# Running the last mixture-of-experts layer of three images inside the next image's attention, and mixing narrow key tiles among full ones

## What is computed

```python
def _L3_attn_ref(x, W1, b1, w2, b2):              # x = layernorm(t)
    f = jnp.einsum('bih,ha->bia', x, W1[:h])      # a: 16
    g = jnp.einsum('bjh,ha->bja', x, W1[h:])
    tt = jnp.tanh(f[:, :, None, :] + g[:, None, :, :] + b1)
    scores = jnp.einsum('bija,a->bij', tt, w2[:, 0]) + b2[0]
    e = jnp.exp(scores) * strictly_lower_triangle
    w = e / (jnp.sum(e, axis=-1, keepdims=True) + 1e-10)
    return jnp.einsum('bij,bjh->bih', w, x)

def _L3_ffn_ref(x, router_w, router_b, expert_w, expert_b):   # x = layernorm(t)
    p = softmax(x @ router_w + router_b)          # 8 experts, the best 2 kept
    top_p, top_i = jax.lax.top_k(p, 2); top_p = top_p / top_p.sum(-1)
    out = jnp.einsum('bnd,edc->bnec', x, expert_w) + expert_b
    return the top_p-weighted sum of the two chosen experts

t = t + _L3_attn_ref(_ln_t(t), ...)
t = t + _L3_ffn_ref(_ln_t(t), ...)
x = t.transpose(0, 2, 1).reshape(4, 128, 64, 64)
```

## Time and profile before

| | us |
|---|---|
| median of three runs | 8764.21 (8760.24 to 8766.25) |
| the profiled execution, its own time | 8764.93 |
| its span, first to last instruction | 8763.1 |
| layers 0 to 2, in the span | 0 to about 4298 |
| attention of layer 3 | 4299.6 to 8378 |
| experts of layer 3 | 8379 to about 8707 |
| way out | about 8709 to 8763 |
| busy share of the span | PE 78%, DVE 73%, ACT 64%, POOL 33% |

### The profile page before, as it was taken

The page is one execution under the profiler, slowest core; times in us unless marked ns, Lnnn a source line. Parts: engine busy times, 40 slices in busy tenths (PEclk is TensorE's granted clock), DMA queues, the critical chain, the costliest instruction groups (busy, mean ns, idle before and its releaser), DMA issues. The chain is left out here.

```text
span 8763.1 us, 103094 instructions
## 1 busy us (share of the span) xinstructions
PE 6793.0 (78%) x37512; PEld 2460.3 (28%) x37512; DVE 6439.3 (73%) x10840; ACT 5612.2 (64%) x4625; POOL 2881.3 (33%) x2218
## 2 busy tenths in 40 slices
PE   8999999987886169948876767777777767767688
PEld 3333333323443123314321213221222212212144
DVE  6777777776754643357888888888888888888766
ACT  3222222214554342234699999999999999999954
POOL 5655566630000300005431223231322223213255
PEclk9999999987887579978989999999999999999998
DMA  1000000001010000000000000000000000000000
GB/s 47 1 1 1 1 1 1 1 4 27 23 26 4 7 0 0 0 0 3 3 1 1 1 1 1 1 1 1 1 1 1 1 1 1 1 1 1 1 3 39
DMA packets 23728, 45.12 MB, mean 5 GB/s; under 512 B 10219, under 2 KB 13421, under 8 KB 22127
## 3 DMA queue, kind: packets, MB, share of 16 engines
q1 hardware_dynamic: 23278, 39.11, 1.5%
HBM read 13.92 MB, written 8.39 MB: 3 GB/s over the span
## 5 line engine op out<-in xcount | busy, mean ns | idle before, releaser
L2350 ACT ACTIVATE aa_tanh<-aa_tanh 128x4096 f32<-128x4096 f32 (+8 forms) x1280 | 3699.3, 2977 | 133.5 <-DVE aa_tanh L2479 133.3
L2479 DVE TENSOR_SCALAR aa_tanh<-aa_f_times,aa_g_bias 128x1024 f32<-128x1024 f32 (+19 forms) x5120 | 3307.6, 718 | 634.2 <-PE aa_scores L2389 633.2
L2389 PE MATMUL aa_scores<-aa_tanh,aa_w_spread 128*32 128x512 f32 (+8 forms) x18432 | 2204.7, 596 | 997.3 <-ACT aa_tanh L2350 996.4
L2318 POOL TENSOR_TENSOR aa_denominators<-aa_denominators,aa_weights 128x1024 f32<-128x1024 f32 (+7 forms) x304 | 771.1, 2536 | 2132.5 <-ACT aa_weights L2341 2122.8
L2389 PEld LDWEIGHTS aa_scores<-aa_tanh,aa_w_spread 128*32 128x32 f32 x18432 | 598.0, 113 | 2454.0 <-ACT aa_tanh L2350 1533.3
L278 POOL TENSOR_TENSOR near_tap_weights<-near_hat_y_mask,near_hat_x 128x1024 f32<-128x1024 f32 x400 | 937.6, 2367 | 473.8 <-PE near_weights_spread L570 465.2
L584 PE MATMUL near_out_sum<-near_weighted,near_w_out 128*128 128x512 f32 x1984 | 997.9, 626 | 24.4 <-DVE near_weighted L357 13.9
L570 PE MATMUL near_weights_spread<-near_tap_weights,near_spread_consts 36*64 36x512 f32 x6272 | 799.3, 609 | 19.3 <-DVE near_weighted L357 12.9
L2403 PE MATMUL aa_out_sum<-aa_weights,aa_normed 128*128 128x512 f32 (+3 forms) x1152 | 598.7, 641 | 148.7 <-POOL aa_weights L2313 148.7
L346 DVE TENSOR_TENSOR near_weighted<-near_weights_spread,near_values 128x1024 f32<-128x1024 f32 x496 | 589.5, 1220 | 147.4 <-PE near_weights_spread L570 147.4
L346 DVE TENSOR_TENSOR near_weights_spread<-near_weights_spread,near_values 128x1024 f32<-128x1024 f32 x288 | 354.0, 1229 | 336.9 <-PE near_weights_spread L570 336.9
(11 more groups left out here) (332 smaller groups left out, 7239.2 us busy)
## 6 DMA issues: line engine op xcount, KB each, us to landing
l_taps<-l_scan_in_out SPq DMA_DIRECT2D x256, 64.0 KB, 2.0
x_rows<-in_x SPq DMA_DIRECT2D x4, 2048.0 KB, 14.3
out_x<-x_rows SPq DMA_DIRECT2D x4, 2048.0 KB, 6.3
qa_x<-in_L_attn_w SPq DMA_DIRECT2D x1, 1024.0 KB, 5.7
L_ffn_expert_w<-in_L_ffn_expert_w SPq DMA_DIRECT2D x2, 512.0 KB
near_spread_consts<-in_deform_consts SPq DMA_DIRECT2D x1, 805.5 KB, 8.2
aa_weights_in<-in_attention SPq DMA_DIRECT2D x1, 577.5 KB
l_weights<-in_mamba SPq DMA_DIRECT2D x1, 557.0 KB
```

The costliest lines, as they stand in the source:

```text
L2318: pool.tensor_tensor(DEN[:, lo:CHUNK], DEN[:, lo:CHUNK], ET[:, n % 2, 0:w], ALU.add).then_inc(den_added, 1)
L2350: a.activation(TH[:, tt, 0:length], TH[:, tt, 0:length], ACT.Tanh).then_inc(th_ready, 1)
L2389: last = t.matmul(sp_[32 * q:32 * q + 32, n % 2, s:e], W2S[:, tt, :], TH[:, tt, o + s:o + e], start=tt == 0, stop=tt == 3, tile_position=( ...
L2479: last = v.tensor_scalar(TH[:, tt, at[q]:at[q] + w - s], FR[:, m % 2, lo + s:CHUNK], GB[:, key:key + 1], None, ALU.add)
```

## The change

The attention stage becomes `attention_and_experts`. It does four things.

1. **The experts of images 0 to 2 run inside the attention of images 1 to 3.** The tables `behind`, `choose` and `raise_gates` give places (n, tt) to new jobs. A *group* is 4 token tiles, eight to an image. Per group: `mt` (4 transposes of the normalised tokens, from GpSimd's `normalize_group`), `ml` (router logits), 8 times `e` (one matmul for 4 experts of one token tile) and `x` (4 transposes back to channels by rows, which replaces the way out). A new group starts every 11 steps (`PERIOD`), so groups overlap and each step of the stretch has one job. They share the two spare banks, in the same rotation, with the own jobs. VectorE does its part four steps of the order later: after `e` it adds all four experts itself (`add_experts`, four chained `scalar_tensor_tensor`), so that it does the work of ScalarE and GpSimd in `moe_layer` too. The gating has the same 18 steps, on 32 columns rather than 128, once per group. Jobs stand only at full key tiles, from the fifth key tile of chunks c = 1 to 3 on: 106 steps of an image, 16 in c = 1, 40 in c = 2, 50 in c = 3.
2. **Diagonal key tiles are spread** (`key_order`): c = 0 takes D0, D7, D1, D6, D2, D5, D3, D4; c = 3 takes 0, D0, 1, 2, 3, D1, 4, 5, 6, D2 and so on; c = 1 and c = 2 likewise. `exponents` comes after step 3 where the tile is narrower than 512.
3. **The norm before the experts is done per image**, with one square root for each, at the start of chunk c = 1 of the next image.
4. `moe_layer` and `to_channels` are left with image 3 alone (32 token tiles, 4 turns of the loop). The outputs of images 0 to 2 are stored by SyncE during the attention, and the expert weights are loaded at its start (three more DMAs, waited for by VectorE before its first instruction on them).

```diff
@@ moe_layer
-        NCK, NGRP = TT // CK, TT // 4
+        NTL = TT - first
+        NCK = NTL // CK
...
+GE = 4 * EX
+STEPS, PERIOD = 18, 11
+NGI = NT // 4
...
-        tiles = [(m, j) for m in range(NM) for j in range((m % NCH + 1) * CT_)]
...
+        def key_order(c):
+
+            if c == 0:
+                return [0, 7, 1, 6, 2, 5, 3, 4]
+            order = list(range(c * CT_))
+            for k in range(CT_ - 1, -1, -1):
+                order.insert(min(c * k + 1, 7 * c), c * CT_ + k)
+            return order
+
+        tiles = [(m, j) for m in range(NM) for j in key_order(m % NCH)]
...
+        behind, choose, raise_gates = {}, {}, {}
+        for b in range(NB - 1):
+            at = [(n, tt) for n, (m, j) in enumerate(tiles) for tt in range(4)
+                  if m // NCH == b + 1 and j < m % NCH * CT_ and 4 <= n - first_of[m] < (m % NCH + 1) * CT_ - 5]
+            for g in range(NGI):
+                G, p = b * NGI + g, PERIOD * g
+                behind[at[p]], behind[at[p + 3]] = ("mt", G), ("ml", G)
+                for k, o in enumerate((1, 2, 4, 5, 7, 8, 9, 10)):
+                    behind[at[p + PERIOD + o]] = ("e", 8 * G + k)
+                behind[at[p + 2 * PERIOD + 6]] = ("x", G)
+                for o, steps in ((4, range(0, 4)), (5, range(4, 8)), (6, range(8, 12)), (9, range(12, 15)), (10, range(15, STEPS))):
+                    choose[at[p + o]] = (G, steps)
+                raise_gates[at[p + 8]] = G
...
@@ gpsimd
+            def normalize_group(G):
+
+                if G % NGI == 0:
+                    pool.wait_ge(sh_ready, 1 + G // NGI + 1)
+                if G:
+                    pool.wait_ge(*full("mt", G - 1))
+                for k in range(4):
+                    t = 4 * G + k
+                    last = pool.tensor_scalar(MU[:, k * P:(k + 1) * P], T[:, t * P:(t + 1) * P], N.scale[:, t:t + 1], SH1[:, t % NT:t % NT + 1], ALU.mult, ALU.add)
+                last.then_inc(mu_ready, 1)
...
@@ scalar
-                    if n and tt == 2:
+                    if n and tt == (2 if w >= BANK else 3):
                         exponents(n - 1)
+                    if (n, tt) in raise_gates:
+                        a.wait_ge(diff_ready, 1 + raise_gates[n, tt] + 1)
+                        a.activation(M1[:, :], M2[:, :], ACT.Exp).then_inc(raised, 1)
+                    if m > NCH and m % NCH == 1 and j == 0 and tt == 1:
+                        N.scalar(a, vv, ss, m // NCH, (m // NCH - 1) * NT, m // NCH * NT)
...
@@ tensor
+            def experts(E):
+
+                G, k, h = E // 8, E % 8 // 2, E % 2
+                t.wait_ge(*bank_before("e", E))
+                t.matmul(bank("e", E), MT[:, G % 2, k * P:(k + 1) * P], EWC[:, 4 * h:4 * h + 4, :].rearrange("p e c -> p (e c)"), start=True, stop=True).then_inc(full("e", E)[0], 1)
...
@@ vector
+            def add_experts(E):
+
+                G, k, h = E // 8, E % 8 // 2, E % 2
+                x = T[:, (4 * G + k) * P:(4 * G + k + 1) * P]
+                v.wait_ge(*full("e", E))
+                if h:
+                    v.wait_ge(*free("e", E - 1))
+                for e in range(4):
+                    c = k * EX + 4 * h + e
+                    ins = v.scalar_tensor_tensor(x, bank("e", E)[:, e * P:(e + 1) * P], GT_[:, G % 2, c:c + 1], x, ALU.mult, ALU.add)
+                    if e < 3:
+                        sum_ch(ins)
+                    else:
+                        ins.then_inc(free("e", E)[0], 1)
...
@@ build
-        additive_attention_layer(nc, d, X, C, N)
-        moe_layer(nc, d, X, C, N, "L3_ffn_", False)
-        to_channels(nc, X, C, out)
+        attention_and_experts(nc, d, X, C, N, out)
+        moe_layer(nc, d, X, C, N, "L3_ffn_", False, TT - NT)
+        to_channels(nc, X, C, out, NB - 1)
```

More of the change, by code:

```diff
@@ new lines, in _ @@
+                    name, at = behind.get((n - 1, tt), (None, 0))
+                    if name == "mt":
+                        keep_group(at)
+                    elif name == "ml":
+                        keep_logits(at)
+                    elif name == "e":
+                        add_experts(at)
+                    elif name == "x":
+                        keep_back(at)
+                    G, steps = choose.get((n - 1, tt), (0, ()))
+                    for step in steps:
+                        gating(G, step)
```

301 lines of the change are left out of this document (229 added, 72 removed).

## The result

The changed kernel takes **8803.55 us** (median of 5 runs, 8798.84 to 8810.66), and the kernel before, on the same chip, 8764.21 (8760.24 to 8768.56). The ratio is **1.0045 [1.0032, 1.0058]**: it is slower by 39 us. The forecast was 8616, faster by 148, with a range to 8735. The time lies outside it, and its sign is the wrong one.

The account below looks back on a forecast made before the run. ScalarE was taken to bound the attention, VectorE having 160 us free per image. 8764.9 - 264.2 (removed work) + 144 (landed jobs) - 40 (spreading) + 8.7 + 3 (small additions) gave 8616 us after a 0.7 median correction; range 8495 to 8735.

Parts of the forecast that it names:

- jobs landed, tables, start: Attention: +144 for experts' jobs landing in three images, +8.7 for square roots with table changes, +3 for the start.
- diagonals spread: Attention, four images: spreading narrow tiles recovers 10 us of ScalarE's loss per image (bounds 0 and 31), -40 in all.
- What goes: Experts stage loses 228.6 us, way out 34.6, norm at the join about 1: together -264.2.
- The slack of the diagonal tiles: Attention: VectorE has 0.85 us free at each diagonal tile, so 12 between the jobs' tiles absorb 10 per image.
- Jobs landed: Images 1 to 3: of VectorE's 151 us added per image, 48 land on the path (bounds 25 and 80), +144.
- The stall of the normalising: Attention: VectorE's fills stand still during GpSimd's `normalize_group`, taken as 1.5 us per group of four token tiles.
- `raise_gates`: Attention: ScalarE waits for VectorE to be two steps further, but is faster there and makes it up; no cost.
- Small additions: Attention: +8.7 for three square roots, +3 for a later start; gates' exps, stores and TensorE's extra work cost nothing.
- All hidden: Rival, attention: VectorE is ahead enough, ScalarE stays the bound and no jobs land; 8477 us, chance 0.15.
- GpSimd's stalls shrink: Rival, attention: GpSimd adds starting while VectorE reads a bank stall nothing; 8576 us, chance 0.15.
- Bank rotation: Rival, attention: TensorE waits for spare banks with scores queued behind, so all 151 us land per image; 8925 us, chance 0.12.
- TensorE's clock: Rival, attention: TensorE's granted clock falls to 0.6 and its work exceeds ScalarE's pace; 8994 us, chance 0.03.

Follow-up runs that it names:

- e1: Kernel before with only its diagonal key tiles spread, no experts' jobs, exps after step 2: 8893.02 us, ratio 1.0149.
- e5: Changed kernel with the exps back after step 2 for narrow tiles too: 8786.90 us, ratio 1.0018.
- e3: Changed kernel with TensorE's `add_tile` issued two steps later, behind the next tile's step 1: 8724.53 us, ratio 0.9951.
- e4: Changed kernel with key tiles in sequence and a new group every 15 steps instead of 11: 8655.85 us, ratio 0.9874.
- e12: e4 with half of VectorE's expert adds left out for images 0 to 2 and the gates' exp three steps later: 8522.31 us, ratio 0.9722.
- e2: Changed kernel with its key tiles in their old sequence, all else as changed: 8718.16 us, ratio 0.9948.
- e6: e4 with the exp of the gates three steps later and the gating's last pieces with it: 8640.85 us, ratio 0.9859.
- e9: e4 with two instead of four of VectorE's adds per expert matmul for images 0 to 2: 8582.39 us, ratio 0.9787.

## Why the prediction was wrong, point by point

With e1 the 34.2 us between the two profiled spans can be split by the prediction's own sum. The end part is measured at 8666.7 and 8367.8; up to there e1 takes 123.9 more than before; the rest of the 298.9 stands with the jobs. That rest has the later exps in it, since e1 has its exps after step 2.

| term | predicted | measured |
|---|---|---|
| experts stage, way out, norm | -264.2 | -264.7 |
| jobs landed, tables, start | +155.7 | +175.0 |
| diagonals spread | -40 | +123.9 |
| sum | -148.5 | +34.2 |

By the medians the parts are 126.6 (e1), 20.7 for the later exps (e5), 156.7 for the jobs (e5 against e1, and 264.7 that go) and -264.7, together 39.3.

**What goes: right.** The pace of 38.10 per set and of 2.88 per turn carried over; 97 and 24 were forecast for what is left, and 98.0 and 22.3 are its windows.

**Diagonals spread: the failed step.** It had 0 to 31 us gained per image, and no loss among its bounds. It counted the fill (2.7) and the narrow tile's cover (under 2), and left out what stands between them. Three things do: the last full step's scores on TensorE (1.92), `add_tile` queued behind them (1.98), and the stall behind GpSimd's add that the late fill then meets (4.91 for four fills of 2.7). The stall was in the same prediction, for full tiles, but not carried to this place. The ordering of TensorE's queue was, for the jobs, but not for `add_tile`. e3 shows the mechanism, since moving these matmuls alone gives back 81, some 55 more than in an order without spreading, and takes the cost in image 0 from 29 to 7. There is one thing more behind it: VectorE's lead of four *steps* was read as a lead of time. Four full steps are 15 us, four steps of D6 about 4. Spread tiles cut the lead each time they come, the narrow tail of the kernel before once per chunk.

**The slack of the diagonal tiles** (0.85 each, from a difference of busy times) was correct as a mean and had no meaning at a place. A mean of free time does not say that a transfer of work between neighbours fits.

**Jobs landed: right in mechanism, near in size.** 48 were foretold to land per image besides 2.9 for the tables. The 175 are 58 for each with the later exps, and 52 without them (156.7); between image 1 and image 0 of the same kernel the chunks c = 1 to 3 grow by 4.5, 24.7 and 20.4, together 49.6. It was a matter of VectorE's free time at the full tiles, as reckoned: e4 shows it by thinning the jobs out and e12 by halving their adds. VectorE's busy time rose by 133.3 us per image and not by 151. Part of that is only how it is counted: one add takes 0.349, but they start 0.38 apart, and the busy time leaves out the gaps between small instructions, by the trace some 12 us in image 1. The 0.366 was about right. The stall of the normalising (1.5 for each of 24 groups, 36) was wrong: the 48 full fills that lie inside an instruction of `normalize_group`, with no add near, took 0.744 each. So a little less work came, and a little more of it landed. The size holds for this order alone: in sequence, e2, the same jobs land 70.

**`raise_gates`: dismissed wrongly.** "ScalarE is the faster one there and makes it up" is true while VectorE is the bound: e6 got 17 of 112 us (three images of 37.2) back. Where it is not, e12 against e9, the same edit is worth 59. In the kernel as changed it was covered, so that this costs the forecast little.

**The exps after step 3** were given no price. They cost 21.

**Small additions.** ScalarE's busy time in image 1 rose by 6.6 (982.4 to 988.9), where the forecast had 2.9 for the tables and eight exps of 0.2. The start was right: from the first DMA of the stage (4294.73 after, 4299.55 before) to ScalarE's first `tanh` (4315.59 and 4316.65) it takes 20.9 us instead of 17.1, 3.8 more where 3 were taken. VectorE now waits for the last of the new loads:

```profile
4301.31 0.68 DVE L2745 TENSOR_SCALAR aa_w_spread<-consts_sb,aa_weights_in 128x32 f32<-128x32 f32 x4 [6.31 <-DMA aa_router_in<-in_experts]
```

**The rivals.** *All hidden* is out: `tanh` waits 92.6 us in the period of one image. *GpSimd's stalls shrink* is out in its size: the fills' busy time over the span rose by 12.7 where it should have fallen. Stalls do fall elsewhere, on small instructions of the gating. VectorE and GpSimd of the kernel after in c = 3 of image 1:

```profile
6107.44 2.13 DVE L2709 TENSOR_SCALAR aa_pick<-aa_max 128x4 f32<-128x4 f32 x1
```

```profile
6107.15 2.40 POOL L2403 TENSOR_TENSOR aa_denominators<-aa_denominators,aa_weights 128x1024 f32<-128x1024 f32 x1 [16.01 <-ACT aa_weights L2444]
```

Four columns took 2.13 us, and both end at 6109.6. The Trainium skill, SBUF — State Buffer, section Who interferes with whom, says that issue order, not the form of the operation, decides which of the two blocks; this row agrees, as the one that began second ended with the first. *Bank rotation* is out: TensorE's matmuls of the experts stood 12.6 us in all for VectorE's adds in that period, and e12, with the same rotation, lands 4 us per image. It named the other side with 0.12, but the way there was another: the slower result came from the term that had been booked as a gain. *TensorE's clock* is out, with 0.93 and 0.94 in these windows against 0.92 before (its factors, 6.6 x 26.5 x 3, make 525 and not 522).

**The range** reached from 8495 to 8735 because the spreading had bounds of 0 and 31 gained. Bounded below nothing it would have needed a price for a wait at each full tile behind a diagonal one (23 in an image), and the trace of before had no such neighbours: its narrow tail, with waits of 2.24 and 2.04, was the nearest row, and it spoke of a loss.

## What to carry to other kernels

When tiles of unequal size are put in another order, walk the slowest neighbour pair through every queue (what stands before the first small operation on each engine), since a look-ahead of so many steps is worth only the time of the steps in it. A mean of free time per tile bounds what can be gained and says nothing of where work fits. Of two edits that go in together, time each alone first: here the jobs gave 48 us and the spreading beside them took 88, and a two-microsecond group of matmuls, moved by two steps, was worth 81.

## What the runs showed that was not expected

- Moving `add_tile` behind the next tile's step 1 gains on each kernel: 81 us with spread tiles, 25 on e4 (8655.85 to 8632.50, each against its own before), 26 on the kernel before.
- An add on GpSimd and the fills beside it stop each other, and either can be the one that stands. Mostly it is VectorE, for about 2 us (2.13 for an instruction of four columns). In e3 an add that began in the middle of a closed row of fills took 18.75 us and the fills kept their pace. What it costs the kernel depends on whether ScalarE waits for the instruction that it meets. That it costs nothing in a row of full tiles and its whole length after a narrow one is read from the traces; no run moves this add alone.
- Adds that read a bank and SBUF take 0.349 us for 128 columns in the mean of 768, though GpSimd was busy 278 of 1099 us beside them. The one that began at 6107.18, 0.03 us after the add on GpSimd shown above, took 0.35; the instruction behind it, on SBUF alone, stood.
- The spreading costs less beside the jobs (88) than alone (127). The place of the exps doesn't explain it: e1 has them after step 2, which is the cheaper place by 21, so that at the same place the gap is larger. What makes it up was not tried apart. Likely reasons are that VectorE is late in the same stretches anyway, and that the narrow tiles between let it catch up: `raise_gates` waits 17.3 us in an image of the kernel after and 47.5 in one of e2.
